# One 125-partition transfer in place of a 112- and a 13-partition one for the memory's rows

## What is computed

```python
# layer 0: one head over the memory
memory_proj = einsum('bme,de->bmd', memory, W_mem)
attn = softmax(einsum('bnd,bmd->bnm', x, memory_proj) / 16)
memory_context = einsum('bnm,bmd->bnd', attn, memory_proj)
x = rmsnorm(x + sigmoid(cat(x, memory_context) @ W_gate.T + b) * memory_context)
# layers 1 and 3 (the gated layers): 16 heads over the memory, masked
k, v = split(memory @ Wkv)
x = x + tanh(attn_gate) * (softmax(mask(q @ k.T)) @ v @ Wo)
x = x + tanh(ff_gate) * (gelu(layernorm(x) @ W1) @ W2)
```

## Time and profile before

| | |
|---|---|
| median of 3 runs | 2456.26 us |
| the profiled execution | 2455.51 us |
| its span | 2453.5 us |
| granted TensorE clock over the span | 0.977 |
| first stage, to the end of the last sums | 118.76 us |
| TensorE (PE) busy | 2332.8 us, 95% |
| VectorE (DVE), ScalarE (ACT), POOL busy | 64%, 52%, 25% |
| DMA: bytes moved, mean rate | 115.96 MB, 47 GB/s |

### The profile page before, as it was taken

One profiled execution on the slowest core, in us unless ns is written; L12 is line 12 of the kernel. 1 busy time (PEld: TensorE's weight loads), 2 busy tenths in 40 slices (PEclk: granted clock), 3 DMA queues, 4 the chain that ended last, 5 costly groups with the idle time before them and its releaser, 6 DMA issues.

```text
span 2453.5 us, 41140 instructions
## 1 busy us (share of the span) xinstructions
PE 2332.8 (95%) x16032; PEld 1894.9 (77%) x16032; DVE 1580.9 (64%) x4256; ACT 1280.9 (52%) x2186; POOL 618.6 (25%) x680
## 2 busy tenths in 40 slices
PE   7978999999999999789999999799999999999999
PEld 4857999999999785356666666446799999999978
DVE  3257777777777557666676676313777777777764
ACT  2135555555555433267777777311555555555543
POOL 0024344443443205100000000001344344344320
PEclk8789999999999999899999999999999999999999
DMA  8720112111110110000000000300011112111010
GB/s 268 194 76 20 45 42 57 33 54 45 42 45 26 53 37 18 26 26 26 27 26 26 26 14 2 123 25 10 20 45 42 45 42 57 37 50 45 26 52 16
DMA packets 36099, 115.96 MB, mean 47 GB/s; under 512 B 4586, under 2 KB 18514, under 8 KB 35906
## 3 DMA queue, kind: packets, MB, share of 16 engines
q1 hardware_dynamic: 33442, 101.04, 13.6%
q10 hardware_dynamic: 2464, 12.29, 2.0%
HBM read 112.40 MB, written 0.92 MB: 46 GB/s over the span
## 4 chain that ended last, share of the span: by engine, by line
PE 85%; DVE 10%; ACT 3%; DMA 1%; issue 1%; ACTq 0%; SPq 0%; DVEq 0%
PE bank L999 19%; PE bank L986 18%; PE bank L1011 12%; PE bank L535 7%; DVE n_scores L1856 5%; PE bank L1737 4%; PE bank L1724 4%; PE bank L1749 3%; PE bank L1961 3%; PE bank L631 2%; PE bank L1973 2%; PE bank L1710 2%; PE bank L829 1%; PE bank L1021 1%; PE bank L619 1%; PE bank L1706 1%
## 5 line engine op out<-in xcount | busy, mean ns | idle before, releaser
L1060 ACT CAST p_T_high<-bank 125x512 fp32r<-125x512 f32 x672 | 350.6, 595 | 517.3 <-PE bank L1011 517.3
L1133 DVE TENSOR_TENSOR p_T_low<-bank,p_T_high 125x512 fp32r<-125x512 f32 x672 | 422.5, 684 | 256.8 <-ACT p_T_high L1060 256.7
L1099 DVE CUSTOM_DVE_ANT_0 scores<-bank,mask 128x500 f32<-128x500 f32 x672 | 418.2, 672 | 1.4 <-PE bank L986 1.4
L1070 ACT ACTIVATE scores<-scores,row_max 128x1500 f32<-128x1500 f32 x224 | 353.4, 1578 | 9.1 <-DVE row_max L1104 9.1
L999 PE MATMUL bank<-p_T_high,keys_nat_high 125*128 125x256 f32 (+1 forms) x1152 | 346.0, 300 | 1.7 <-ACT inverse L1067 1.7
L999 PE MATMUL bank<-p_T_high,keys_nat_low 125*128 125x256 f32 (+1 forms) x1152 | 346.3, 301 | 0.0
L999 PE MATMUL bank<-p_T_low,keys_nat_high 125*128 125x256 f32 (+1 forms) x1152 | 346.2, 300 | 0.0
L1011 PE MATMUL bank<-ident,scores 128*125 128x128 f32 x2688 | 331.0, 273 | 2.3 <-ACT scores L1070 2.3
L1011 PEld LDWEIGHTS bank<-ident,scores 128*125 128x125 f32 x2688 | 318.5, 187 | 5.0 <-ACT scores L1070 4.8
L1856 DVE CUSTOM_DVE_ANT_0 n_scores<-bank,n_zeros 112x500 f32<-112x500 f32 x384 | 237.4, 674 | 131.2 <-PE bank L1724 131.2
L986 PE MATMUL bank<-keys_T_high,q_stage_high 128*128 128x500 f32 x672 | 282.3, 420 | 9.8 <-DVE q_stage_low L1076 6.9
(11 more groups left out here) (223 smaller groups left out, 3473.3 us busy)
## 6 DMA issues: line engine op xcount, KB each, us to landing
ctx_T<-in_ctxT SPq DMA_DIRECT2D x32, 750.0 KB, 4.3
ctx_nat<-in_ctx SPq DMA_DIRECT2D x32, 672.0 KB
q_and_o<-in_ctxT SPq DMA_DIRECT2D x16, 750.0 KB, 10.2
n_ctx_T<-in_ctxT SPq DMA_DIRECT2D x16, 750.0 KB, 4.1
q_and_o<-in_ctx ACTq DMA_DIRECT2D x16, 672.0 KB
mask_bytes<-in_mask SPq DMA_DIRECT2D x32, 187.5 KB, 5.2
weights<-in_L_W SPq DMA_DIRECT2D x4, 1024.0 KB, 10.0
ctx_nat<-in_ctx SPq DMA_DIRECT2D x32, 78.0 KB
```

The costliest lines, as they stand in the source:

```text
L1060: e.copy(PTs[0][g % 2][0:KP, 4 * c:4 * c + 4, lo:lo + 128], psum[3 + c][0:KP, :].rearrange("p (k r) -> p k r", k=4)).then_inc(s_eh, 1)
L1070: e.activation(SB[s % 2], SB[s % 2], ACT.Exp, bias=mx[:, s % 4, 3:4], accum_out=mx[:, s % 4, 4:5]).then_inc(s_ex, 1)
L1099: e.tensor_tensor_reduce(out=SB[u % 2][:, c * CHK:(c + 1) * CHK], in0=psum[c][:, 0:CHK], in1=mb[:, c * CHK:(c + 1) * CHK], scale=1.0, scal ...
L1133: e.tensor_tensor(low, psum[3 + c][0:KP, :].rearrange("p (k r) -> p k r", k=4), high.bitcast(F32), ALU.subtract).then_inc(s_el, 1)
```

## The change

Both loops over (0, 112) and (112, 125) go; one transfer of 125 partitions for each batch takes their place. The waits ask for 16 in place of 32. Nothing else changes.

```diff
@@ act_l0_keys
-                for lo, hi in ((0, 112), (112, KP)):
-                    e.dma_start(kn0[b % 4][lo:hi, :], ctx_rows[b, lo:hi, :]).then_inc(s_l0_kn[b % 4], 16)
+                e.dma_start(kn0[b % 4][0:KP, :], ctx_rows[b]).then_inc(s_l0_kn[b % 4], 16)
@@ pe_l0
-                        on.wait_ge(s_l0_kn[b % 4], 32 * (b // 4 + 1))
+                        on.wait_ge(s_l0_kn[b % 4], 16 * (b // 4 + 1))
@@ Cross
             def keys_loaded(self, b):
-                return s_knl[b % 2], 32 * (self.b0 // 2 + b // 2 + 1)
+                return s_knl[b % 2], 16 * (self.b0 // 2 + b // 2 + 1)
@@ sp_cross
-                for lo, hi in ((0, 112), (112, KP)):
-                    e.dma_start(kn_raw[b % 2][lo:hi, :], ctx_rows[b, lo:hi, :]).then_inc(s_knl[b % 2], 16)
+                e.dma_start(kn_raw[b % 2][0:KP, :], ctx_rows[b]).then_inc(s_knl[b % 2], 16)
```

## The result

The kernel after takes 2495.09 us, the median of four runs (2493.41 to 2500.44), beside 2456.35 for the kernel before: a ratio of 1.0165, with a 95% interval of 1.0145 to 1.0185. The forecast was 2494.6 us. The profiled execution took 2493.95 us, its span is 2492.0 us and its mean clock 0.968.

The account below looks back on a forecast made before the run. The prediction took the first stage as balanced between TensorE (busy 95% of the span) and transfers. 2455.51 + 38.3 for the first stage, 0 for gated layers and issues, gave 2493.8; the median's 0.75 made 2494.6 us, range 2470 to 2530.

Parts of the forecast that it names:

- Five engines: Natural-row transfers: 125 partitions go over 5 DMA engines, 25 rows each, the largest divisor up to 16; chance 0.74.
- 3.149 MB at 23.1 GB/s: First stage: bytes on one of the five engines from 15.5 us take 136.3 us, so the last rows land at 151.8.
- 130 to 150 GB/s at a share near 0.4: Sign for first-stage windows: this DMA rate and share in place of 277 GB/s and 1.03.
- The last batch's half of the sums at the lower clock: End of first stage: 5.2 us of sums behind the last rows, ending at 157.0 in place of 118.76, +38.3 us.
- The five engines stay fed: First stage: 13.3 us of rows still to move cover the 2.8 to 5.2 us of sums and 1.7 us issue and start.
- The sign that I had given: First stage: TensorE's sums wait for natural rows in nearly every unit, 30 to 60 us in place of 1.8.
- The gated layers cost nothing: Gated layers: rows land 2.5 us later, but POOL's 2.90 us idle and 11 us more cover it; 28 batches cost 0.
- The removed issues: ACT in the first stage: 16 issues fewer, some 0.4 us each, nothing on the path, so 0.
- Half clock as the bound: Rival, first stage: TensorE at half clock takes 18.2 us a unit, ending at 165, +46, 2503 us; chance 0.13.
- Sixteen engines: Rival: 125 rows go over 16 engines, at most 8 each, 2456 us, not slower; chance 0.08.
- One engine: Rival: one engine takes all 125 rows, 33 us a batch, +410 in the first stage, above 3200 us; chance 0.02.
- the main case: Whole kernel: five engines bound by their bytes in the first stage, +38.3 us, ends +12 and +109; chance 0.74.

Follow-up runs that it names:

- 113 on one: Gated layers alone split into transfers of 113 and 12 partitions, first stage as in the kernel before: 2742.43 us, ratio 1.1162.
- 120 and 5: Kernel before with the first stage's natural rows split into transfers of 120 and 5 partitions in place of 112 and 13: 2461.17 us, ratio 1.0018.
- 100 and 25: Kernel before with the first stage's natural rows split into transfers of 100 and 25 partitions in place of 112 and 13: 2473.17 us, ratio 1.0079.
- 95 and 30: Kernel before with the first stage's natural rows split into transfers of 95 and 30 partitions in place of 112 and 13: 2494.3 us, ratio 1.0155.
- the first stage alone: Single transfer of 125 partitions in the first stage only, gated layers with 112 and 13 as in the kernel before: 2497.34 us, ratio 1.0168.
- 61 rows on an engine: Gated layers alone split into transfers of 122 and 3 partitions, first stage as in the kernel before: 2456.32 us, ratio 0.9996.
- The kernels with one transfer of 128: Kernel before with one wide transfer of 128 partitions for each batch but the last: both stages 2439.35 us (0.9938), first stage only 2438.77 us (0.9931).
- the version that beats both: Kernel before with one transfer of 128 partitions for each batch but the last, in the first stage only: 2438.77 us, ratio 0.9931.

## Why the prediction was right

- **Five engines**. Shown by 2080 and 274 packets and the DMA share of 0.32. The largest divisor up to 16 fits each count tried: 125 on 5 and 113 on one by themselves (the latter by its rate of 25 GB/s), and the pairs by the sum of their completions, 15 + 5 for 120 and 5, 10 + 5 for 100 and 25, 5 + 15 for 95 and 30.
- **3.149 MB at 23.1 GB/s.** The last 24 matmuls began at 150.34, predicted 151.8. The mean from 15.5 us on is 3.149 / 134.8 = 23.4 GB/s. But it is a mean of two rates: 26 GB/s with the natural rows alone (131 / 5), less beside transposed batches, 183 / (16 x 0.59) = 19.4 from 50 to 90 us. I had foreseen 130 to 150 GB/s at a share near 0.4 for the whole stage; of its second half the rate came, 130 GB/s, at a share of 0.32. That the rate of transposed batches on 16 engines came out as the mean is partly luck.
- **The last batch's half of the sums at the lower clock**: 5.2 us predicted, 5.40 measured. The end at 157.0 came at 155.76. That only half of a unit's sums stood behind the last row is in part luck: with the first stage alone the last row landed at 151.91, the predicted 151.8, and the end was 162.44.
- **The five engines stay fed.** From 100 to 140 us, where the natural rows are nearly alone, the share is 0.32 or 0.33 at 130 to 132 GB/s in each stretch of 10 us, five engines at work all the time; it is 0.31 from 60 to 70 and 0.29 in the last 10 us. Where transposed batches move beside them a mean over 16 engines can't tell the five. The sign that I had given, a wait for rows in nearly every unit, 30 to 60 us together, came short: 28.9 us in every second unit.
- **The gated layers cost nothing.** The landing after 8.4 us was 8.6, POOL's wait 9 us was 9.3, and the change there alone gives 0.9997. The cover that I read from POOL's order holds with 61 rows on an engine and fails with 113.
- **The removed issues** were not tried by themselves. The kernels with one transfer of 128 remove them too and gain 17 us; by the stretches most of that is the time of a row, and up to the 1.8 us that I had priced at the stage's start may be the issues.
- **The rivals.** Half clock as the bound: not of the stage as a whole. The sums took 5.57 or 10.8 us for 48, the clock had a mean of 0.67 at 50 to 90 us, and yet every second unit ended with a wait for rows. But it took the end of the stage in the profile of the first stage alone, 5 us more, and in that of 95 and 30; the 162.44 is nearer to this rival's 165 than to my 157.0, with the rows landed where I had them. Sixteen engines: refuted for 125. Had they come, I gave the time as 2456; the wide transfer shows that it can also be 2439, since I had priced only the rows on an engine and not the time of a row. One engine: not for 125, but for 113. Its price of +410 us left out the start and the transposed memory; in the terms of the main case, 12.98 MB at 23.1 GB/s, it is some +464, which changes nothing about "above 3200".

## What to carry to other kernels

Ahead of joining or splitting a transfer, factor its partition count: the packets of a queue less its rows tell how many engines its transfers used, and the fullest engine's rows times the time of a row tells about how long a transfer takes. That time is no constant: here it went from 0.26 to 0.42 us with the split. A count with no divisor near 16 is better rounded up to 128, where the rows beyond are harmless, than joined as it is. And ask where the load is covered: the same transfer cost 1.7% of the kernel in a stage whose DMA engines were full, and nothing in two layers where rows that landed 18.2 us after their issue still came in time.

## What was not expected

- In the first stage the same 6144-byte row took 0.263 us on 5 engines, 0.266 us in a transfer of 128 partitions, and 0.37 to 0.42 us in every other split over 15 or 16 engines. The kernel before moved 271 GB/s where the wide one moved 420, both at a full share. With it the version that beats both came: 2438.77 us.
- With one engine holding 113 rows, SP's issues of natural rows took up to 24.65 us in place of 0.99 at most, at the start of the layer with two batches in the queue, and 9.12 us for the pair at 249.87; with 61 rows on each of two, up to 15.57 us. A lopsided transfer can hold up the queue that issues it.
- The runs of one kernel spread over some 12 us, and the clock at the stage's end is part of it. The kernel before ran from 2449.03 to 2460.89 us in 17 runs beside the first of the experiments, the two with wide transfers from 2436.49 to 2447.97. In the profile that I have of each of the latter, one with a span of 2436.7 us stayed at full clock to the stage's end and one of 2446.0 us fell to half for the last two sums, 9.29 and 8.36 us in place of 5.57 and 5.56. That this is the whole of the spread was not tried.
